# Max pooling that reads the gathered planes directly, two buffers for the row maxima, and GpSimd's 72 tiles written out

## The reference, cut to what matters

```
def _L1_conv_ref(x, w1, b1, w2, b2):          # x is already normalised by groups
    gap = jnp.mean(x, axis=(2, 3))
    hmid = relu(einsum('bc,ec->be', gap, w1) + b1)
    s = relu(einsum('be,ce->bc', hmid, w2) + b2)
    q_s = clip(floor(s), 0, 5);  q_b = q_s + 1
    pools = stack([maxpool_same(x, k) for k in (1, 3, 5, 7, 9, 11, 13)])
    s_out, b_out = pools[q_s], pools[q_b]     # for each plane (image, channel)
    return (s - q_s) * b_out + (q_b - s) * s_out + x
x = x + _L1_conv_ref(_gn(x), ...)
```

## Time and profile before

| what | value |
|---|---|
| median of 3 runs | 4385.2 us (4382.19 to 4385.34) |
| the profiled execution, its own time | 4390.08 us |
| its span | 4388.4 us |
| TensorE busy in the span | 3910.1 us (89%) |
| VectorE busy | 3365.5 us (77%) |
| GpSimd busy | 2213.8 us (50%) |
| ScalarE busy | 1894.2 us (43%) |
| moved by DMA | 781.08 MB, mean 178 GB/s |
| tiles with planes in the second part | 67 (of 72), by the count of L546 and L682 |

### The profile page before, as it was taken

One profiled execution on the slowest core, in us unless ns is written; L12 is line 12 of the kernel. 1 busy time (PEld: TensorE's weight loads), 2 busy tenths in 40 slices (PEclk: granted clock), 3 DMA queues, 4 the chain that ended last, 5 costly groups with the idle time before them and its releaser, 6 DMA issues. The chain is left out here.

```text
span 4388.4 us, 76845 instructions
## 1 busy us (share of the span) xinstructions
PE 3910.1 (89%) x23656; PEld 2177.6 (50%) x23657; DVE 3365.5 (77%) x3528; ACT 1894.2 (43%) x2964; POOL 2213.8 (50%) x1793
## 2 busy tenths in 40 slices
PE   5999999999999999999999947799888888888885
PEld 3666666566666666666666633333333333333332
DVE  5777777777777777777777657699766799999993
ACT  3444445454544444444454314444333334333332
POOL 3555555554555555555555414355544444555442
PEclk9999999999999999999999958899998999999887
DMA  4445445454444544454553344544555566665551
GB/s 185 157 172 179 146 164 179 172 176 166 171 152 169 179 160 157 172 185 164 177 180 110 109 104 186 198 171 170 203 229 227 203 241 231 240 239 215 216 215 51
DMA packets 252235, 781.08 MB, mean 178 GB/s; under 512 B 98150, under 2 KB 98150, under 8 KB 229990
## 3 DMA queue, kind: packets, MB, share of 16 engines
q1 hardware_dynamic: 219600, 417.85, 27.6%
q0 software_dynamic: 32288, 358.95, 21.2%
HBM read 428.22 MB, written 409.08 MB: 191 GB/s over the span
## 5 line engine op out<-in xcount | busy, mean ns | idle before, releaser
L1072 DVE TENSOR_TENSOR arena<-arena 128x2048 f32<-128x2048 f32 (+5 forms) x539 | 1442.3, 2694 | 266.0 <-ACT arena L684 232.0
L447 POOL TENSOR_TENSOR arena<-arena 128x512 f16<-128x512 f32 x512 | 651.1, 1277 | 861.3 <-ACT arena L605 859.7
L1412 PE MATMUL psum<-arena 128*128 128x512 f32 x1072 | 608.1, 651 | 297.5 <-ACT arena L704 215.1
L456 POOL TENSOR_TENSOR arena<-arena 128x512 f32 (+1 forms) x512 | 640.2, 1272 | 298.0 <-ACT arena L617 292.0
L1241 PE MATMUL psum<-arena 128*128 128x512 f16 x2048 | 776.4, 379 | 1.0 <-ACT arena L617 1.0
L1242 PE MATMUL psum<-arena 128*128 128x512 f16 x2048 | 776.3, 379 | 0.0
L1243 PE MATMUL psum<-arena 128*128 128x512 f16 x2048 | 776.2, 379 | 0.0
L1218 PE MATMUL psum<-arena 128*128 128x256 f16 (+1 forms) x6344 | 718.9, 271 | 34.3 <-DVE arena L817 21.1
L682 ACT ACTIVATE arena<-arena 128x4096 f32 x67 | 242.4, 3618 | 1055.6 <-issue 1055.6
L603 ACT ACTIVATE arena<-arena,gbias,grstd 128x512 f32 (+1 forms) x512 | 413.7, 808 | 631.5 <-PE psum L1243 515.6
L1218 PEld LDWEIGHTS psum<-arena 128*128 128x128 f16 x6344 | 592.2, 99 | 121.8 <-DVE arena L817 29.0
(11 more groups left out here) (161 smaller groups left out, 3877.3 us busy)
## 6 DMA issues: line engine op xcount, KB each, us to landing
arena<-in_x SPq DMA_DIRECT2D x64, 2048.0 KB, 13.0
wide_planes<-arena SPq DMA_DIRECT2D x128, 1024.0 KB, 8.8
y_planes<-arena SPq DMA_DIRECT2D x64, 2048.0 KB, 7.7
arena<-arena SPq DMA_DIRECT2D x1536, 8.0 KB, 1.8
arena<-wide_planes,arena POOLq DMA_INDIRECT x72, 9.8
arena<-plane_records,arena POOLq DMA_INDIRECT x67, 4.2
arena<-y_planes,arena POOLq DMA_INDIRECT x67, 9.2
out<-arena POOLq DMA_INDIRECT x67, 7.9
```

Source lines behind the costliest of these rows:

```text
L447: pool.tensor_tensor(gl[:, ct, slot], g32[:, ct % 2, :], gh[:, ct, slot], ALU.subtract).then_inc(s_gl, 1)
L456: pool.tensor_tensor(y, y, relu[:, o % 2, :], ALU.add).then_inc(s_added, 1)
L1072: ins = dve.tensor_tensor(dst, a, b, ALU.max)
L1412: pe.matmul(dst, diag[:, s, 0, :], bufs[:, u, b * CW:(b + 1) * CW], start=True, stop=False)
```

## The change

ScalarE's `pad_plane`, `ypad`, `s_ypad`, `src_at` and the one-column index copies go. `source` gets a second buffer, each with two rows of lowest values above and below. VectorE reads the gathered planes (classes 0 and 1) or `source` (classes 2 to 5) itself and takes care of the edge columns by short extra operations. It waits for `gathered` or `sourced` itself. GpSimd gathers from `wide_planes` two tiles ahead, after a wait for `s_rows`, its 72 steps are written out, with the index columns addressed directly. ScalarE clears the records after use. VectorE's loop body holds four tiles. The diff, cut to its core:

```diff
-                pool.sem_inc(s_issue, 1)
-                pool.memset(recs_in[:, b, :], 0.0)
-                pool.tensor_copy(idx[:, b:b + 1], ids_i[:, bass.ds(t, 1)]).then_inc(s_idx, 1)
-                pool.wait_ge(s_idx, t + 1)
-                pool.sem_inc(s_issue, 1)
+                planes = bass.IndirectOffsetOnAxis(ap=ids_i[:, t:t + 1], axis=0)
...
             def gather_source(t, b):
-                if not (isinstance(t, int) and t == 0):
-                    pool.wait_ge(s_ypad, t)
-                    pool.wait_ge(sourced, t * 16)
-                pool.tensor_copy(src_idx[:, b:b + 1], src_ids[:, bass.ds(t, 1)]).then_inc(s_src, 1)
-                pool.wait_ge(s_src, t + 1)
+                if t >= 2:
+                    pool.wait_ge(s_rows, t - 1)
+                    pool.wait_ge(sourced[b % 2], t // 2 * 16)
+                pool.indirect_dma_start(out=source_flat(b % 2), out_offset=None, in_=wide_dram[:, :],
+                                        in_offset=bass.IndirectOffsetOnAxis(ap=src_ids[:, t:t + 1], axis=0),
...
             def step(t, u):
+                if t + 2 < NT:
+                    gather_source(t + 2, (u + 2) % BUFS)
+                    if t >= 2:
+                        pool.wait_ge(written[(u + 2) % BUFS], ((t - 2) // BUFS + 1) * 16)
                     gather(t + 2, (u + 2) % BUFS)
+                if t >= 1:
                     scatter(t - 1, (u - 1) % BUFS)
+            pool.memset(recs_in, 0.0).then_inc(s_recs_clear, 1)
+            pool.wait_ge(s_recs_clear, 1)
             gather(0, 0)
             gather_source(0, 0)
             gather(1, 1)
+            gather_source(1, 1)
+            for t in range(NT):
+                step(t, t % BUFS)
...
             def diagonals(t, u):
+                act.wait_ge(gathered[u], turns_done(t, u))
...
+                act.wait_ge(s_diag, t + 1)
+                act.activation(recs_in[:, u, :], ident[:, 0:REC], ACT.Copy, scale=0.0)
...
-                if not (isinstance(t, int) and t + 1 >= NT):
-                    pad_plane(t + 1, (u + 1) % BUFS)
...
                 if k < 2:
-                    window(cols, cols_mid, lambda e: inner[:, :, e::2], 1, signal=s_rows)
+                    op(half, plane[:, :, 0::2], plane[:, :, 1::2])
+                    op(inner[:, :, 0:W:W - 1], half[:, :, 0:32:31], half[:, :, 0:32:31])
+                    op(inner[:, :, 2::2], half[:, :, 1:], plane[:, :, 1:W - 2:2], wait=False)
+                    op(inner[:, :, 1:W - 1:2], half[:, :, 0:31], plane[:, :, 2::2], wait=False, signal=s_rows)
                 elif k == 2:
                     window(source_rows, rows_mid, small_rows, k, signal=s_rows)
                 elif k < 5:
-                    op(inner, shifted(2 - k), shifted(k - 2), signal=s_rows)
+                    d = k - 2
+                    op(inner[:, :, 0:d], wides[:, :, d:2 * d], wides[:, :, 0:1].to_broadcast([P, H, d]))
+                    op(inner[:, :, W - d:W], wides[:, :, W - 2 * d:W - d],
+                       wides[:, :, W - 1:W].to_broadcast([P, H, d]), wait=False)
+                    op(inner[:, :, d:W - d], wides[:, :, 0:W - 2 * d], wides[:, :, 2 * d:W], wait=False, signal=s_rows)
                 else:
-                    core = cols_mid(half_m, 0, 32)
-                    op(core, cols(-2, 32), cols(3, 32))
-                    op(inner[:, :, 0::2], core, cols(-3, 32))
-                    op(inner[:, :, 1::2], core, cols(4, 32), wait=False, signal=s_rows)
+                    op(half[:, :, 1:31], wides[:, :, 0:W - 5:2], wides[:, :, 5::2])
+                    op(half[:, :, 0:32:31], wides[:, :, 0:W - 3:W - 4], wides[:, :, 3:W:W - 4], wait=False)
+                    op(inner[:, :, 0:3:2], half[:, :, 0:2], half[:, :, 0:2])
+                    op(inner[:, :, W - 3:W:2], half[:, :, 30:32], half[:, :, 30:32], wait=False)
+                    op(inner[:, :, 4::2], half[:, :, 2:], wides[:, :, 1:W - 4:2], wait=False)
+                    op(inner[:, :, 1:W - 4:2], half[:, :, 0:30], wides[:, :, 4:W - 1:2], wait=False, signal=s_rows)
...
-                    dve.wait_ge(s_ypad, t + 1)
...
+                            if lo < 2:
+                                dve.wait_ge(gathered[u], loaded)
+                            else:
+                                dve.wait_ge(sourced[u % 2], (t // 2 + 1) * 16 if wide_loaded is None else wide_loaded)
...
-            for t in range(2):
-                tile(t, t)
-            with dve.Fori(1, NT // 2) as g:
-                for s in range(2):
-                    tile(g * 2 + s, s)
+            for u in range(BUFS):
+                tile(u, u)
+            with dve.Fori(1, NT // BUFS) as g:
+                for u in range(BUFS):
+                    tile(g * BUFS + u, u, (g + 1) * 32, (g * 2 + (u // 2 + 1)) * 16)
```

More of the change, by code:

```diff
@@ L36 @@
 LOWEST = -3.4028234663852886e38
-PADC = 4
 PADY = 2
@@ L212, in build @@
         tnum = v(NT)
-        tmod_i = v(NT).bitcast(i32)
-        tmod, sel, unsel, src_f = (v(NT) for _ in range(4))
+        sel, unsel = (v(NT) for _ in range(2))
         not_first = v(1)
@@ L295, in build @@
         s_rec = sem("s_rec")
+        s_recs_clear = sem("s_recs_clear")
         s_onehot = sem("s_onehot")
@@ L299, in build @@
         s_pads = sem("s_pads")
-        s_idx = sem("s_idx")
         gathered = [sem(f"gathered{b}") for b in range(BUFS)]
-        sourced = sem("sourced")
-        s_src = sem("s_src")
+        sourced = [sem(f"sourced{b}") for b in range(2)]
         written = [sem(f"written{b}") for b in range(BUFS)]
-        s_ypad = sem("s_ypad")
         s_rows = sem("s_rows")
@@ L550, in scatter @@
                 with pool.Else():
-                    pool.dma_start(no_out[bass.ds(t, 1), :], bufs[0:1, b, 0:REC]).then_inc(written[b], 16)
+                    pool.dma_start(no_out[t:t + 1, :], bufs[0:1, b, 0:REC]).then_inc(written[b], 16)
             def step(t, u):
-                if not (isinstance(t, int) and t + 1 >= NT):
[L556 to L560, removed]
+                if t + 2 < NT:
+                    gather_source(t + 2, (u + 2) % BUFS)
+                    if t >= 2:
+                        pool.wait_ge(written[(u + 2) % BUFS], ((t - 2) // BUFS + 1) * 16)
                     gather(t + 2, (u + 2) % BUFS)
-                if not (isinstance(t, int) and t < 1):
+                if t >= 1:
                     scatter(t - 1, (u - 1) % BUFS)
+            pool.memset(recs_in, 0.0).then_inc(s_recs_clear, 1)
+            pool.wait_ge(s_recs_clear, 1)
             gather(0, 0)
@@ L969, in sort_planes @@
                 link(dve.tensor_tensor(fb, score, cls, ALU.subtract))
-                dve.wait_ge(s_iota, 4)
+                dve.wait_ge(s_iota, 3)
                 dve.tensor_copy(lane, lane_i)
@@ L1058, in sort_planes, with pools @@
                 dve.tensor_copy(ids_i, ids).then_inc(s_sorted, 1)
-            OWN = 22
-            def pools(t, s, k):
-                used = [0]
+            OWN = 20
+            def pools(t, u, k):
+                used, s = [0], u % 2
                 def op(dst, a, b, wait=True, signal=s_own):
@@ L1097, in window @@
                     op(dst(1), mid(core, 0, 32), src(1 + r, 32), wait=False, signal=signal)
[L1099 to L1105, removed]
+                plane = bufs[:, u, :].rearrange("p (h w) -> p h w", w=W)
+                wides = source[:, s, PADY:PADY + H, :]
+                half = half_m.rearrange("p (h w) -> p h w", w=36)[:, :, 0:32]
                 def rows(i, n):
@@ L1145, in pools, with tile @@
                 dve.sem_inc(s_own, OWN - used[0])
-            def tile(t, s):
+            def tile(t, u, loaded=32, wide_loaded=None):
                 cls_t = dve.value_load(cls_i[0:1, bass.ds(t, 1)], min_val=0, max_val=NCLS)
                 def waits():
-                    dve.wait_ge(s_ypad, t + 1)
                     if not (isinstance(t, int) and t < 2):
```

43 lines of the change are left out of this document (11 added, 32 removed).

## The result

The changed kernel takes 4274.85 us (median of 4 runs, 4270.62 to 4282.81) against 4385.27 (4 runs); the ratio is 0.9751, with a 95% interval of 0.9734 to 0.9768. That is 110 us less, where 191 had been forecast, and at the very end of the range. The profiled execution has a span of 4274.8 us against 4388.4, and the forecast's sum for the span was 4196.6: 78 us went somewhere else.

The account below looks back on a forecast made before the run. The padding's wait chain was taken to bound classes 0 and 2, VectorE class 5. Start 2625.9, class periods 1512.5, then 26.2 and 32 gave a 4196.6 us span, adjusted to 4194 us; range 4168 to 4275.

Parts of the forecast that it names:

- the ring of the padding: Classes 0 and 2: padding, results, store, next gather and next padding wait in turn, 21.7 us a tile in class 0.
- The edge operations: VectorE's extra short operations: +0.16 us a tile in classes 0 and 1, +0.3 in 3 and 4, +0.46 in 5.
- The end: After VectorE's last operation: 26.2 us to the last full tile's store, then 32 us for empty tiles and final landing.
- Rival (a): Second part: transfers become the bound at about 240 GB/s, 133 us more, 4327 us; chance 0.09.
- Code: VectorE's four-tile loop body, 17 trips: jumps back cost 0 to 36 us, taken as 0 because the preceding operation hides 2.1.
- The row from the first part: Profile row of VectorE's first-part loop: 25.0 us of idle time in 12 trips, 2.1 each.
- the bound of 36 us: Upper end for jumps back in VectorE's second-part loop, 17 trips with none of the 2.1 us each hidden.
- GpSimd: Order of waits and issues in GpSimd's steps: class 0 store landing in 7.9 us, planes ready 6 us early.
- rival (b): GpSimd's strict order binds: class 0 at 18 us a tile, class 2 at 23.6, total 4273 us; chance 0.15.
- Its other half: Class 2: GpSimd's issues, class reads and a store landing take 23.6 us a tile, 38 us more in all.
- the hand-overs: Passing a tile between VectorE and TensorE with two result buffers: 0.4 us each, two per two periods in class 0.
- the period of classes 0 and 1: Time per tile: 14.25 us in class 0 from VectorE, TensorE and passing times, 22.9 in class 1 from VectorE.

Follow-up runs that it names:

- The body of 302 instructions: The changed kernel with VectorE's loop body cut from four tiles to two, plane buffer addressed through a register: 4307.2 us, ratio 0.9821.
- both cured: The changed kernel with VectorE's 72 tiles written out and GpSimd's store of tile t-1 ahead of the gather of t+2: 4214.9 us, ratio 0.9604.

## Why the prediction was wrong

**What was right.** That the ring of the padding bound classes 0 and 2 and that TensorE is next in class 2: 20.7 us forecast, 20.60 with VectorE written out, at a granted clock of 1.00. The edge operations: 25.64 us a tile forecast in class 4, 25.65 measured; in class 5 284.0 us for ten tiles less the two stalls, 284.3 forecast. The end (55.7 against 58.2), and the start to 2.3 us: VectorE waited 10.4 us for its own planes, where 12.7 had been counted; the other 4.9 us by which it began earlier lie in the first part. Rival (a) fell: 287 GB/s, where it put the most at about 240 and the forecast took 290, left TensorE busy throughout.

**The step that failed first** is *Code*: "I take 0, since the operation ahead of the jump is 4.4 us long in classes 1 to 5, and hides 2.1". The profile after has 57.5 us of it in 15 places: 1.8 to 2.8 us at nine trips in classes 1, 3, 4 and 5, 5.3 to 9.0 at five trips of classes 1 to 3, and one of 2.5 in class 0. The row from the first part was the right one; its loop has 453 instructions, so it too is longer than the bodies that were held. Even the bound of 36 us, with nothing hidden, was too low. The wrong step was to hide it: the row is idle time, what remained behind other work, and a last operation of 4.4 us left 2.8 us of idle time in class 4. Why some trips lose 5 to 9 us isn't shown. Written out, VectorE gives back 47 us. The Trainium skill (Runtime: NRT & Kernel Launch, Instruction fetch mechanics) speaks of such a stall at a taken branch out of the two pages held, and prefers full unrolling: the runs agree with the second. With the first they agree only in part. The body of 302 instructions stalled at 23 of 34 trips, though two of that section's pages of 256 instructions have room for it unless it lies across three; where it lies wasn't determined.

**The second** is in *GpSimd*: the sum took a landing of 7.9 us for the store, from a kernel in which the store was issued alone, and left 6 us of room. In the new order the store stands 2.4 us behind a gather of 2.1 MB and lands after 13.2. The wait for it stands ahead of the next gather and the next store, so stores can't overlap: landing and about 5.5 us of issues make 18.7 us a tile in place of 14.25. Class 0 was 34 us over the sum. That is rival (b) as named ("the ring would close again, through `written`"; 18 us in class 0), with 0.15 too small a chance. Its other half didn't happen: in class 2 GpSimd's issues never bound.

With both cured, 4214.9 us are left against 4194. Class 0 still takes 15.6 us a tile (VectorE from 2625.61 to 2797.17), 15 us above the sum in all. Class 1 (to 3060.01) is 11 us above it: VectorE waits there for TensorE some 2.2 us at every second tile, and the sum took class 1 from VectorE's work alone. Whether the hand-overs and a lower granted clock make these waits wasn't tested. So the third step that failed, for 26 us, is the period of classes 0 and 1, and its cause stays open.

## What to carry to other kernels

In these runs a loop jumped back free of charge while no code was loaded for it, and lost 2 to 3 us or more at a trip when it was. Look for instruction packets in the loop's stretch of the kernel at hand and of the changed one: if they appear, count a stall per trip, and don't hide it behind the last operation. Here writing the loop out was cheaper than a longer body. Where one engine issues all DMAs in order, ask of each wait what is queued behind it: a wait for the landing of a store ahead of the next store makes stores serial, and the landing to count with is the one behind the gather just issued, not the one of a queue that was empty.

## What the runs showed of the hardware

- VectorE's loops with bodies of 242 and 266 instructions loaded no code from 3000 to 4200 us; with bodies of 302, 530 and 570 there were 124, 67 and 92 instruction packets (about ten of the 124 and of the 92 are GpSimd's). The idle time at a trip was 2.5 to 2.8 us in class 4 and 1.8 to 2.0 in class 5, nearly the same for two tiles as for four, and up to 9.0 in classes 1 to 3. Straight code with forward branches, 72 tiles of it, had 47 packets there, GpSimd's ten among them, and not one stall that the profile shows.
- In class 0 a store of 2.1 MB landed 7.9 us after its issue with no gather of planes just ahead, and after 13.2 us with one issued 2.4 us before it.
- Taking the copy off GpSimd, and with it 2.1 us between a store and a gather, gave nothing in class 0: the padding that waits for the gather moved from 7.0 us behind its issue to 9.2.
